# The one-hots of attention_sums: every other pair of groups from ScalarE, the pairs between from VectorE

## The reference, cut to what matters

```python
ex = jnp.exp(a - amax[dst])
den = jax.ops.segment_sum(ex, dst, num_segments=n)
alpha = ex / (den[dst] + 1e-16)
...
agg = jax.ops.segment_sum(alpha * h, dst, num_segments=n)
```

## Time and profile before

| | us |
|---|---|
| median of three executions | 6455.58 |
| profiled execution, its own time | 6450.41 |
| its span, first to last instruction | 6448.6 |
| attention_sums, first activation of L1624 to the last add | 3761.3 to 4065.2 |
| busy over the whole span: PE, DVE, POOL, ACT | 4844.0, 4815.1, 4226.7, 2313.8 |

### The profile page before, as it was taken

How to read it: one execution, slowest core, us unless ns; L and a number is a source line. 1 busy time by engine, 2 the same in 40 slices (tenths; PEclk the granted TensorE clock), 3 DMA queues, 4 the chain that set the end, 5 groups by cost and what they waited for, 6 DMA issues and landing times. The chain is left out here.

```text
span 6448.6 us, 162454 instructions
## 1 busy us (share of the span) xinstructions
PE 4844.0 (75%) x45499; PEld 3772.4 (58%) x45500; DVE 4815.1 (75%) x10999; ACT 2313.8 (36%) x6999; POOL 4226.7 (66%) x4249
## 2 busy tenths in 40 slices
PE   6666767388888888888888769876666677777775
PEld 3444445277777777777777757644444454444444
DVE  5777776488888898888888764577777756666665
ACT  1000002266666666666666567410000020000011
POOL 5777775177767777777777347277777727777771
PEclk8888888699999999999999989888888887777777
DMA  3333332133333333333333247222222212222221
GB/s 107 92 93 92 92 92 69 42 90 94 92 89 92 89 92 92 90 92 91 90 92 89 67 148 229 62 73 73 72 72 72 72 40 70 69 69 69 69 69 35
DMA packets 401394, 545.14 MB, mean 85 GB/s; under 512 B 144934, under 2 KB 283318, under 8 KB 401180
## 3 DMA queue, kind: packets, MB, share of 16 engines
q0 software_dynamic: 193920, 331.22, 21.0%
q1 hardware_dynamic: 207388, 212.84, 11.3%
HBM read 464.79 MB, written 78.90 MB: 84 GB/s over the span
## 5 line engine op out<-in xcount | busy, mean ns | idle before, releaser
L805 POOL DMA_INDIRECT e_rows<-tab,e_idx x2424 | 2291.2, 945 | 811.0 <-issue 690.4
L1074 POOL DMA_INDIRECT acc<-tabx,a_idx x1616 | 1686.5, 1044 | 869.9 <-issue 467.9
L850 PE MATMUL e_wps<-e_w,e_hidT 64*128 64x192 f32 (+1 forms) x4848 | 790.6, 460 | 874.6 <-DVE e_hidT L921 871.5
L850 PEld LDWEIGHTS e_wps<-e_w,e_hidT 64*128 64x128 f32 x4848 | 538.2, 250 | 1079.1 <-DVE e_hidT L921 965.4
L835 PE MATMUL e_win<-e_feat,e_ohy 128*32 128x96 f32 (+1 forms) x19392 | 1025.6, 330 | 27.1 <-DVE e_feat L915 25.6
L835 PEld LDWEIGHTS e_win<-e_feat,e_ohy 128*32 128x32 f32 x19392 | 707.2, 131 | 455.9 <-issue 293.9
L906 DVE TENSOR_TENSOR e_feat<-e_wps,e_rows 128x256 f32<-128x256 f32 x606 | 257.5, 425 | 834.5 <-DMA e_rows<-tab,e_idx 761.2
L915 DVE TENSOR_TENSOR e_feat<-e_wps,e_rows 128x384 f32<-128x384 f32 (+1 forms) x1616 | 720.5, 498 | 0.0
L1137 PE MATMUL a_c<-acc,a_buffer 128*128 128x64 f32 (+1 forms) x4848 | 624.9, 272 | 121.6 <-ACT a_buffer L1115 121.6
L824 ACT ACTIVATE e_idx<-src 128x4 int32 (+1 forms) x606 | 123.2, 204 | 1606.4 <-DMA e_rows<-tab,e_idx 1585.1
L1137 PEld LDWEIGHTS a_c<-acc,a_buffer 128*128 128x128 f32 (+1 forms) x4848 | 590.5, 192 | 143.6 <-issue 143.6
(11 more groups left out here) (252 smaller groups left out, 7851.2 us busy)
## 6 DMA issues: line engine op xcount, KB each, us to landing
h_d<-a_buffer SPq DMA_DIRECT2D x202, 322.0 KB, 2.5
s_hin<-h_d SPq DMA_DIRECT2D x202, 322.0 KB, 3.5
e_rows<-tab,e_idx POOLq DMA_INDIRECT x2424
e_ein<-in_e64T SPq DMA_DIRECT2D x202, 128.0 KB
acc<-tabx,a_idx POOLq DMA_INDIRECT x1616
a_ein<-in_e_h SPq DMA_DIRECT2D x202, 64.0 KB
e_ein<-in_e16T SPq DMA_DIRECT2D x202, 32.0 KB
tab<-p_rows SPq DMA_DIRECT2D x36, 160.0 KB
```

Of the source, the lines that this page charges most:

```text
L805: pool.indirect_dma_start(out=rows[:, s, t, :], out_offset=None, in_=k.tab0, in_offset=bass.IndirectOffsetOnAxis(ap=idx[:, s, t:t + 1], ax ...
L850: mm = pe.matmul(wps[:, e, 2 * u + j, 0:WC], hidT[half, edges], w2[half, :], start=True, stop=True)
L1074: pool.indirect_dma_start(out=rows[:, b, q, :], out_offset=None, in_=table, in_offset=bass.IndirectOffsetOnAxis(ap=idx[:, b, end, q:q + 1] ...
```

## The change

`apart` shrinks to one half. ScalarE now makes only the pair of s = 0 (half 0), once in a turn of four groups, and signals `oh_act`. VectorE makes the pair of s = 2 (half 1) with one comparison `is_equal` of 128x256 between `iota`, of which it first makes a copy in a PSUM bank, and the keys in SBUF, and signals `oh_dve`. The first of these comparisons stands ahead of VectorE's memset; each later one stands behind the step s = 3 of its loop, for groups g + 3 and g + 4, with a wait until GpSimd has read the half (`ohx_ready`). GpSimd waits for `oh_act` at s = 0 and for `oh_dve` at s = 2.

```diff
--- before.py
+++ after.py
@@ -1581,10 +1581,11 @@
         ohx = sb("s_ohx", [P, U, TPG, H, NB])
         rel, key, off, mod = (sb("s_" + part, [P, TPG]) for part in ("rel", "key", "off", "mod"))
         win = ps("s_win", [P, U, 512])
-        apart = sb("s_apart", [P, 2, 2 * TPG, NB])
+        apart = sb("s_apart", [P, 2 * TPG, NB])
         h_in = [sem(f"s_h_in{s}") for s in range(R)]
-        cleared, apart_ready = sem("s_cleared"), sem("s_apart_ready")
-        oh_ready, ohx_ready, win_ready, added = sem("s_oh_ready"), sem("s_ohx_ready"), sem("s_win_ready"), sem("s_added")
+        cleared, apart_ready, iota_ready = sem("s_cleared"), sem("s_apart_ready"), sem("s_iota_ready")
+        iota = ps("s_iota", [P, 512])[:, 0:NB]
+        oh_act, oh_dve, ohx_ready, win_ready, added = sem("s_oh_act"), sem("s_oh_dve"), sem("s_ohx_ready"), sem("s_win_ready"), sem("s_added")
         ahead_in = sem("s_ahead_in")
         group_done = sem("s_group_done")
         more_ohx, more_win, more_link = sem("s_more_ohx"), sem("s_more_win"), sem("s_more_link")
@@ -1610,8 +1611,10 @@
             @block.gpsimd
             def _(pool):
                 def step(g, s, i):
-                    if s % 2 == 0:
-                        hold(pool, k, oh_ready, i * 2 + s // 2 + 1)
+                    if s == 0:
+                        hold(pool, k, oh_act, i + 1)
+                    if s == 2:
+                        hold(pool, k, oh_dve, i + 1)
                     if not isinstance(g, int) or g >= U:
                         hold(pool, k, added, g - U + 1)
                         hold(pool, k, group_done, g - U + 1)
@@ -1624,21 +1627,18 @@
                 act.activation(k.acc_all[:, half:k.NBLK * W], k.ones[:, 0:1].to_broadcast([P, k.NBLK * W - half]), ACT.Copy,
                                scale=0.0).then_inc(cleared, 1)
 
-                def ones_at(first, half, pair):
-                    for j in range(2 * TPG):
-                        ins = act.activation(apart[:, half, j, :], k.iota[:, :], ACT.Abs, scale=-1.0,
-                                             bias=k.key_all[:, bass.ds(first * TPG + j, 1)])
-                    ins.then_inc(apart_ready, 1)
-                    hold(act, k, apart_ready, pair + 1)
-                    act.activation(oh[:, half, :, :, :].rearrange("p u t n -> p (u t) n"), apart[:, half, :, :], ACT.Relu, scale=-1.0,
-                                   bias=k.ones[:, 0:1]).then_inc(oh_ready, 1)
-
                 def step(g, s, i):
-                    if s % 2 == 0:
+                    if s == 0:
                         if not isinstance(g, int) or g >= U:
                             hold(act, k, ohx_ready, g - 2)
-                            hold(act, k, oh_ready, i * 2 + s // 2 - 1)
-                        ones_at(g, s // 2, i * 2 + s // 2)
+                            hold(act, k, oh_act, i)
+                        for j in range(2 * TPG):
+                            ins = act.activation(apart[:, j, :], k.iota[:, :], ACT.Abs, scale=-1.0,
+                                                 bias=k.key_all[:, bass.ds(g * TPG + j, 1)])
+                        ins.then_inc(apart_ready, 1)
+                        hold(act, k, apart_ready, i + 1)
+                        act.activation(oh[:, 0, :, :, :].rearrange("p u t n -> p (u t) n"), apart[:, :, :], ACT.Relu, scale=-1.0,
+                                       bias=k.ones[:, 0:1]).then_inc(oh_act, 1)
 
                 rounds(act, n, step, lo=U, U=U)
 
@@ -1669,6 +1669,13 @@
             @block.vector
             def _(v):
 
+                def ones_at(first):
+                    v.tensor_tensor(oh[:, 1, :, :, :].rearrange("p u t n -> p (u t) n"), over(iota, 1, 2 * TPG),
+                                    over(k.key_all[:, bass.ds(first * TPG, 2 * TPG)], 2, NB), ALU.is_equal).then_inc(oh_dve, 1)
+
+                v.tensor_copy(iota, k.iota[:, :]).then_inc(iota_ready, 1)
+                v.wait_ge(iota_ready, 1)
+                ones_at(2)
                 v.memset(k.acc_all[:, 0:half], 0.0).then_inc(cleared, 1)
                 cur = v.alloc_register("s_block")
                 words = [v.alloc_register(f"s_dve_word{u}") for u in range(U)]
@@ -1716,6 +1723,9 @@
                                 link(add(at, o, j))
                             v.nop()
                         v.sem_inc(group_done)
+                        if s == U - 1 and inside(g + 3, n):
+                            hold(v, k, ohx_ready, g + 1)
+                            ones_at(g + 3)
 
                 rounds(v, n, step, lo=U, U=U)
```

## The result

The changed kernel takes 6466.68 us (median of 20 executions, 6461.95 to 6473.5) against 6456.73 (20 executions, 6451.65 to 6464.74): ratio 1.0015, 95% interval 1.0009 to 1.0021. It is slower by 10 us, or 0.15%. The profiled execution has a span of 6462.4 us against 6448.6, and a mean granted clock of 0.885 against 0.886.

The account below looks back on a forecast made before the run. The prediction took VectorE's queue to bound the stage: four added queue instructions, 0.40 us a turn, 50 times, gave 20 us; ScalarE's saving, GpSimd's wait, ramp and end gave 0. 6455.58 + 20 = 6476, range 6460 to 6498.

Parts of the forecast that it names:

- The bound: Stage attention_sums: the order in which VectorE's queue can be worked off sets the turn of 5.76 us.
- The windows that stood ready 2.2 us: Before VectorE's add of s = 0: TensorE's window was ready 2.2 us, so the wait named "PE" is not one.
- inner part of 6468 to 6486: Whole kernel: the forecast of 0.25 to 0.6 us more a turn, +12.5 to +30 us, chance 0.64.
- Four queue instructions, 0.40 us a turn: VectorE behind s = 3: hold value, hold, key address and comparison, 0.10 us each, 50 times, 20 us.
- the other 43 instructions: VectorE's queue in one turn, besides the 0.95 us register load: they fill 4.81 us, 0.112 each.
- the loop's code grows by five instructions: Rival, fetch at the loop's branch: each turn waits for its code, at most +95, 6551; chance 0.02 together with clock.
- The new ring: VectorE's comparison, GpSimd's s = 2, TensorE, VectorE's add of s = 3: 0.2 us shorter than the queue's turn, hidden.
- TensorE as the bound: Rival: VectorE really waits for ScalarE and GpSimd; freed, TensorE sets 1.34 us a group, 19 us less, 6437; chance 0.08.
- No difference: Rival: VectorE's four instructions cost 0.1 to 0.25 us a turn, hidden by the loop's branch, +5 to +12; chance 0.13.
- Slower by more: Rival: comparison counts in full or GpSimd's new wait lasts longer, turn 6.4 to 6.6 us, +32 to +41; chance 0.13.
- Clock: Rival: granted clock of 0.50 in the stage, +247, 6703; expected 1.00; chance 0.02 together with code fetch.
- a step s = 2 or s = 3 longer than 1.13 (the ring binds): Sign against the forecast in VectorE's adds; steps of 1.01, 1.01, 1.13 should stay unchanged, only the last grow by 0.4.

Follow-up runs that it names:

- the four increments: Kernel before the change with four semaphore increments behind step s = 3 of VectorE's loop, nobody waiting for them: stage 298.8 us, turn 5.92.
- the comparison four times as large: Kernel before the change with a 128x1024 comparison on VectorE whose result nobody reads, taking 1.22 us: turn 5.81 us, stage 293.3.
- the unread comparison: Kernel before the change with VectorE's iota copy and comparisons added, written to a spare tile nobody reads: stage 293.1 us, turn 5.82.

## Why the prediction was right or wrong

**The bound: right, but by 0.03 us a turn.** VectorE's queue sets the stage of the kernel before, not its datapath and not ScalarE. Behind the first groups none of its holds for a window waits (0.12 us from L716 to L85 throughout), the four increments cost 0.09 us each in full, and the comparison four times as large cost nothing. ScalarE's halved work gave nothing, as costed. But the prediction gave TensorE 5.3 of 5.76 us, from two loads 1.33 apart, and that was too little: with its loop branch and its one long step it needs 5.73. The windows that stood ready 2.2 us were those of s = 0 alone; that of s = 3 was ready 1.0 ahead. The queue of VectorE was the bound, and the next one lay right behind it.

**The sign and the range: right; the size: half.** I said 20 us and 6476, and it was 10 us and 6467, inside the range but below its inner part of 6468 to 6486. Three steps stand behind that.

- *Four queue instructions, 0.40 us a turn.* There were three: the value of the hold needed no instruction of its own, because the register with g + 1 was still there from the wait for the window. They cost 0.26. The price for one instruction, 0.10, was about right (0.09 measured).
- *The sum took the other 43 instructions as fixed.* They were not. With the code a few instructions further on they needed 0.21 us less. Nothing in the prediction named this; "the loop's code grows by five instructions" appeared only as a cost. 50 x (0.26 - 0.21) = 2.5 us is what the queue adds, not 20.
- *"The new ring is 0.2 us shorter than the queue's turn, hence hidden, but only just."* The ring was sized at 5.98 us within one turn. It closes over two, through six groups of TensorE with the loop branch (0.5 us) and the long step (0.27), which I had not counted, and takes 11.90. Two turns of the queue that I compared it with should have taken 12.32 (2 x 6.16) and came out as 11.62 (2 x 5.81). Half of 50 turns wait 0.29: 7.3 us.

2.5 + 7.3 = 9.8, against 9.4 between the adds. The runs split it much the same: 3.1 us from the kernel before to the unread comparison (293.1), 6.3 from there to the changed kernel. So most of the loss is the wait that I had called hidden, and the term that I had counted nearly cancelled. The result came nearer to the forecast than its steps deserve.

**The rivals.** TensorE as the bound with 6437: out, the turn got longer. Its price was also wrong, by the 5.3 us above: with 5.73 a turn there were 2 us to gain and not 19. *No difference*, 6461 to 6468: the time, +0.15%, lies there, within the 0.2% that I had set for it, but not by its mechanism; the queue instructions did not slip into the branch's gap, which the four increments show. *Slower by more*, with the comparison's run counted: out by the run with 1.22 us. Clock: the granted clock is 1.00 from 3840 to 3960 us as before, and a product of TensorE takes 310 ns against 311 in the earlier trace rows. The register load stayed at 956 ns. Among the signs that I had named as making me wrong was "a step s = 2 or s = 3 longer than 1.13 (the ring binds)": the step of 1.34 is just that.

The Trainium skill's page Perfetto Trace Analysis (section DVE / Act Engine Instruction) says that the sequencer is free for the next instruction once it has pushed one into the wait queue. The run with 1.22 us, which added nothing, agrees. The Trainium skill's page Runtime: NRT & Kernel Launch (section Instruction fetch mechanics) says that a taken branch whose target lies outside the two pages held has to fetch it. The gaps here, 0.1 us, move with one or two instructions, and no run here shows whether such a page is behind them.

## What to carry to other kernels

An engine with 48% busy time can still be the bound: look whether the thing it is said to wait for was ready long before, in every step and not only in one, and if so count the instructions of its queue, some 0.1 us each, register work and semaphores included. Work handed to such an engine costs by its queue entries and not by its run; work that another engine then waits for closes a ring, and a ring has to be compared with the shortest turn that may come out, over as many turns as the longest loop on it has, with the loop branches of every engine. The second bound deserves the same care as the first: one pair of loads 1.33 us apart hid a TensorE that needed 5.73 of 5.76 us. When a difference of some tenths of a per cent is at stake, a control that only moves the code belongs among the experiments.

## What the hardware showed that I had not expected

- Gaps between queue instructions depend on where the code lies: the same loop of VectorE takes 5.76 us a turn, 5.69 or 5.74 one or two instructions further on, and 5.56 four or eight further on (3.5%). One gap of 0.12 us moves back in the loop by one instruction for each instruction put ahead of it.
- TensorE's loop branch adds 0.5 us between two products (1.84 against 1.33), and one more step of eight has 0.27 us in which TensorE waits for nothing (1.60). Eight groups so need 11.46 us, and by that alone, once VectorE's comparison made it start late, the turns alternated between 5.81 and 6.10.
- A register load of four words takes 0.95 us of VectorE's queue whether its datapath is busy or not.
